# Layer 1's context stage placed between the shared and the routed experts, and statistics per tile in the last stage

## The chip, the cores and the metric

The kernel runs on one core of a Trainium2 chip. The metric is device time in microseconds (us) from launch to the end of the core's program; lower is better. A core has five engines that each run their own instructions in order: PE (matrix products, with a separate row PEld for its weight loads), DVE (vector), ACT (scalar functions), POOL (GpSimd) and SP (which here only starts transfers). They wait for each other through semaphores alone.

## The reference

Input: x, 64 sequences of 64 tokens of 128 features; a context of 64 tokens of 256 features per sequence (two halves of 128); a mask of patch lengths; two pairs of gates.

```python
x = x + tanh(g_xattn[0]) * attention(layernorm(x), context)
x = x + tanh(g_ffn[0])   * moe(layernorm(x))
x = x + tanh(g_xattn[1]) * depool(layernorm(x), context, mask)
x = x + tanh(g_ffn[1])   * linear_experts(layernorm(x))
```

- attention: 16 heads of 8 features over 64 own and 64 context keys, softmax, projection.
- moe: a shared gated FFN (128 to 256 and back), plus the one best of 8 experts of the same shape per token, fed with the token times the sigmoid of its best logit.
- depool: rmsnorm(x) times W_in plus b_in, plus a row of a decaying sum over the rms-normalised first half of the context (the rms is over all 256 features); which row is the token's "plug", a running count of patch ends that comes from the mask.
- linear_experts: the sum of the two best of 8 matrices applied to the token, and their biases.

## The kernel before

The program is written without a scheduler: each engine's order stands in the code, and every wait is put in by hand. The 4096 tokens are NT = 32 tiles of 128 tokens (two sequences). A stage is a pipeline: `walk` (L64) calls a step function that asks `stage(lag)` for the tile that is `lag` steps behind the newest, so one step of an engine touches several tiles at different points. The first steps and the drain are unrolled, the rest is a loop. A semaphore S[...] counts the tiles that have passed a point; `done()` waits for a tile, `freed()` for a buffer to be free again.

The stages in order of time, with their place in the profiled execution:

1. **Attention**, to 280 us. It takes 32 steps and a drain of 11 (the pipeline's depth is 11). It ends per tile with layer 0's second layernorm (the result is kept in VALL, which is XN2), its transpose (XNT) and the 8 router logits (LG). In a step ACT does in this order: copy onT of an older tile (L564), copy qc (L568), four exponentials (L557), copies xrT and XNT (L603, L604), and last, copy oS (L614). PE waits for onT (`pe.wait on_kept`) ahead of both the logits product L1129 and the projection L1132, and behind these stand the scores L1075 that the next exponentials read.
2. **Sort**, 280 to 292 us, on DVE from L844: best expert, its rank among the tokens of the same expert, and so a row of a buffer in which each expert's tokens stand together (NS = 40 tiles of 128 rows). ACT takes sigmoids and scales the 32 tiles (L631).
3. **Scatter and shared FFN**, 292 to 357 us. POOL issues one indirect DMA per tile (L466) that writes its rows to the sorted place. Beside it the shared FFN runs on 8 chunks of 4 tiles: PE lifts a chunk (L1206, L1207: four products of 128x512), ACT takes silu (L640), DVE multiplies (L890), PE takes it down (L1216: eight 128x128 products), DVE adds it to X (L895). In the same steps ACT squares the context, 8 activations a chunk (L646), whose sums are the rms. DVE compares patch ends with places (L900) and POOL turns them to plugs (from L487), writes them out and reads them back over 64 rows.
4. **Routed experts**, 357 to 447 us: 40 sorted tiles; SP loads (L368) and stores (L371), PE transposes (L1239) and multiplies (L1234 and others).
5. **Gather and context stage**, 447 to 519 us. POOL issues 32 indirect DMAs (L514) that fetch each tile's rows back. Beside it, per tile: DVE scales the context by its rms (L936), PE applies the decay (L1271), ACT copies the result (L674), DVE compares the plugs with the row number (L941, a 128x128 matrix of zeros and ones), PE picks with it (L1277), DVE adds the bias into DP, which is CV (L945); then DVE adds the gathered tile to X (L949) and takes its mean and variance (L955, L959), which ACT copies for the next step (L678).
6. **Root chain**, 519 to 522 us: once all 32 tiles have their moments, DVE forms the roots' arguments (L974 and on), ACT takes Sqrt (L682, with a table load), DVE inverts and refines.
7. **Last stage**, 522 to 652 us: 32 tiles, depth 9. ACT normalises (L690), PE multiplies by W_in (L1289), POOL adds DP (L527), DVE adds (L991) and takes moments; POOL takes variance and root (L531, L534), DVE normalises (L998), PE computes logits (L1309 with others); DVE finds the two best, PE applies all 8 experts (L1319) and DVE masks them (L1021); SP stores (L382).

SP also issues, after attention, the loads of all weights that are used later (L352) and five writes of zeros over the sorted buffer (L360); POOL multiplies these weights by their gates (L455 to L458) before the scatter.

## Time and profile before

| what | value |
|---|---|
| time, median of 3 runs | 609.88 us (608.68 to 610.11) |
| the profiled execution: its span | 652.3 us; no other time is given for it |
| PE busy / its weight loads | 535.1 us (82%) / 378.2 us (58%) |
| DVE busy | 426.2 us (65%) |
| ACT busy | 320.0 us (49%) |
| POOL busy | 247.1 us (38%) |

The page's slices of the span (16.3 us each; a digit is tenths of busy time, PEclk tenths of the full TensorE clock) show the stages: the sort is the gap in PE at slice 18, the gather the low PE values from slice 27 to 31.

```profile
PE   2699999999999999648638989995206479999998
DVE  4789898889898986375114323335218867888885
ACT  2477877777777776385234334442002442333320
POOL 5324444444444434378743700004760052232320
PEclk9799999999999999869868799998556859999999
```

The profile's rows are one execution, taken by the hardware profiler. A row of the timeline has the start in us from the span's start, the duration, the engine, the line, the operation, its output and input, how often, and in brackets the idle time before it and what ended it. "issue" and "remote" stand there when nothing in the program that the profile shows was waited for.

### The profile page before, as it was taken

What the parts mean: (1) busy time and instruction counts of PE and PEld (TensorE: products, weight loads), DVE (VectorE), ACT (ScalarE), POOL (GpSimd) and SP (SyncE); (2) the same over time, 40 slices, a digit from 0 to 9 for tenths busy, and PEclk for the clock granted to TensorE, in tenths of its full rate; (3) what the DMA queues carried; (4) which work ended last, traced back from release to release, by engine and by line L of the source; (5) the groups of instructions that cost most, each with busy time, mean ns of one, the idle gap of its engine ahead of it and who ended that gap; (6) DMA issues with size and microseconds to landing.
All of it is one profiled execution on the core that took longest, in us unless ns stands there. A gap on an engine that the chain in (4) does not pass through costs nothing. (4 is left out here: it accounts for less than half of the span.)

```text
span 652.3 us, 19574 instructions
## 1 busy us (share of the span) xinstructions
PE 535.1 (82%) x5898; PEld 378.2 (58%) x5899; DVE 426.2 (65%) x1504; ACT 320.0 (49%) x1039; POOL 247.1 (38%) x551
## 2 busy tenths in 40 slices
PE   2699999999999999648638989995206479999998
PEld 1366666666666666415325545554105359999997
DVE  4789898889898986375114323335218867888885
ACT  2477877777777776385234334442002442333320
POOL 5324444444444434378743700004760052232320
PEclk9799999999999999869868799998556859999999
DMA  8400000000000000821110252211110000000000
GB/s 278 168 4 3 4 3 4 1 1 1 1 1 1 1 2 4 325 85 45 52 49 6 52 115 64 67 53 41 52 52 0 0 2 14 21 16 20 16 22 25
DMA packets 24188, 27.24 MB, mean 42 GB/s; under 512 B 5144, under 2 KB 20816, under 8 KB 23504
## 3 DMA queue, kind: packets, MB, share of 16 engines
q1 hardware_dynamic: 21712, 21.40, 10.0%
q0 software_dynamic: 2432, 5.28, 3.2%
q8 instruction: 24, 0.39, 0.3%
q14 instruction: 20, 0.16, 0.1%
HBM read 17.06 MB, written 9.45 MB: 41 GB/s over the span
## 5 line engine op out<-in xcount | busy, mean ns | idle before, releaser
L740 DVE TENSOR_REDUCE negm<-PS 128x4 f16<-128x512 f32 x128 | 85.3, 687 | 2.3 <-PE PS L1062 1.3
L557 ACT ACTIVATE pexp<-PS 128x512 f32<-128x512 f32 x128 | 79.0, 625 | 7.3 <-PE PS L1075 6.7
L1319 PE MATMUL PS<-w,vp 128*128 128x128 f32 x512 | 64.3, 280 | 0.0
L514 POOL DMA_INDIRECT VALL<-sorted_y,posu x32 | 30.5, 953 | 83.5 <-DMA sorted_y<-arena 74.1
L1319 PEld LDWEIGHTS PS<-w,vp 128*128 128x128 f32 x512 | 61.4, 196 | 0.1
L1062 PE MATMUL PS<-kt,arena 128*64 128x128 f16 x1024 | 53.7, 229 | 5.7 <-DVE negm L740 5.1
L1089 PE MATMUL PS<-pexp,vp 128*32 128x64 f32 x2048 | 54.1, 225 | 2.8 <-ACT pexp L557 0.2
L923 DVE TENSOR_TENSOR pexp<-PS,oS 128x256 f32<-128x256 f32 x40 | 17.0, 424 | 55.5 <-ACT oS L656 55.5
L406 POOL TENSOR_TENSOR ve<-mv,epsc 128x1 f32<-128x1 f32 x32 | 6.4, 199 | 120.0 <-DVE mv L775 120.0
L1234 PE MATMUL PS<-rgu,xsT 128*128 x80 | 46.7, 667 | 3.5 <-ACT xsT L661 2.0
L1062 PEld LDWEIGHTS PS<-kt,arena 128*64 128x64 f16 x1024 | 33.3, 111 | 27.6 <-issue 11.8
L1089 PEld LDWEIGHTS PS<-pexp,vp 128*32 128x32 f32 x2048 | 34.3, 109 | 22.6 <-issue 11.9
L1075 PE MATMUL PS<-arena,kt 128*128 128x256 f16 x256 | 44.5, 276 | 0.0
L1271 PE MATMUL PS<-stack,cst 128*128 128x128 f32 x64 | 18.4, 380 | 31.0 <-DVE stack L936 16.6
L466 POOL DMA_INDIRECT sorted_x<-VALL,posu x32 | 34.0, 1063 | 13.9 <-issue 13.9
L1021 DVE TENSOR_TENSOR vp<-PS,xnT 128x1024 f32<-128x1024 f32 x32 | 38.7, 1209 | 0.8 <-PE PS L1296 0.8
L789 DVE COPY arena<-qc 32x512 f16<-32x512 f16 x128 | 37.0, 289 | 1.3
L1097 PE MATMUL PS<-ident,stack 128*128 128x128 f16 x384 | 34.2, 228 | 2.6 <-DVE stack L804 2.6
L704 ACT CAST mask1T<-PS 8x128 f32<-8x128 f16 x32 | 8.1, 254 | 55.7 <-PE PS L1324 55.7
L531 POOL TENSOR_TENSOR ve<-mv,epsc 128x1 f32<-128x1 f32 x32 | 6.1, 189 | 71.1 <-DVE mv L1012 71.1
L1271 PEld LDWEIGHTS PS<-stack,cst 128*128 128x128 f32 x64 | 11.9, 234 | 36.1 <-DVE stack L936 20.2
L568 ACT COPY qc<-PS 128x512 f16<-128x512 f16 x32 | 18.7, 585 | 27.8 <-PE PS L1097 27.8
(204 smaller groups left out, 1363.6 us busy)
## 6 DMA issues: line engine op xcount, KB each, us to landing
sorted_x<-zeros SPq DMA_DIRECT2D x5, 512.0 KB, 10.1
xs<-sorted_x SPq DMA_DIRECT2D x40, 64.0 KB, 1.8
sorted_y<-arena SPq DMA_DIRECT2D x40, 64.0 KB, 1.6
arena<-mT SPq DMA_DIRECT2D x128, 1.0 KB
rgu<-in_rt_gate_up_dram SPq DMA_DIRECT2D x1, 2048.0 KB
out_dram<-X SPq DMA_DIRECT2D x32, 64.0 KB, 1.5
X<-in_x_dram SPq DMA_DIRECT2D x1, 1536.0 KB, 8.6
CK<-in_ctx_k_dram SPq DMA_DIRECT2D x1, 1536.0 KB, 11.8
```

Source lines behind the costliest of these rows:

```text
L466: pool.indirect_dma_start(out=sorted_x, out_offset=bass.IndirectOffsetOnAxis(ap=posu[:, t:t + 1], axis=0), in_=XN2[:, t * D:t * D + D], in ...
L514: pool.indirect_dma_start(out=XN2[:, t * D:t * D + D], out_offset=None, in_=sorted_y, in_offset=bass.IndirectOffsetOnAxis(ap=posu[:, t:t + ...
L557: nc.scalar.activation(pexp[:, j, :], PS[:, 2 + j % 2, :], ACT.Exp).then_inc(S["exped"], 1)
L740: dve.tensor_reduce(negm[:, a.par, :, j], PS[:, j % 2, :].rearrange("p (h k) -> p h k", h=HG), AX.X, ALU.max, negate=True).then_inc(S["max ...
L789: last = dve.tensor_copy(qbd[rows, s.slot, :, hg, :], qc[rows])
L1021: dve.tensor_tensor(z[:, m.par], PS[:, 4:6, :].rearrange("p b (e t) -> p (b e) t", t=P), xnT4[:, m.slot, :].unsqueeze(1).to_broadcast([P, ...
L1062: last = nc.tensor.matmul(PS[64 * b:64 * b + 64, j % 2, hg * P:hg * P + P], qbd[:, a.slot, j, hg, 64 * b:64 * b + 64], kt[:, a.slot, b, j, :],
L1075: last = nc.tensor.matmul(PS[:, 2 + j % 2, 256 * g2:256 * g2 + 256], kt[:, b.slot, seq, g, :], qbd[:, b.slot, g, :, SEQ * seq:SEQ * seq + ...
L1089: last = nc.tensor.matmul(PS[32 * hg:32 * hg + 32, 7, g * P + SEQ * seq:g * P + SEQ * seq + SEQ], vp[:, b.par, seq, g * HG + hg, :], pexp[ ...
L1097: last = nc.tensor.transpose(bank16(bank)[:, col + g * P:col + (g + 1) * P], stack[:, s.par, w, g * HG:g * HG + HG, :].rearrange("p h c -> ...
L1234: nc.tensor.matmul(PS[:, 2 + s.par, :], xsT[:, s.par, :], rgu[:, ds(e_lift * (2 * FF), 2 * FF)], start=True, stop=True).then_inc(S["e_lift ...
L1319: nc.tensor.matmul(PS[:, 6 + y.par, 0:D], z[:, y.par, e, :], w1[:, e * D:e * D + D], start=(e == 0), stop=False)
```

## The change

1. The 11 late loads and the five zero writes go from SP (after attention) to POOL, at the end of its attention steps for tiles 2 to 11: two loads a step, and in the first five a zero write. The bias and the gain of the context's halves are now loaded four times side by side (ginit4, binB4), so there are 17 loads. Five small memsets are added at POOL's start.
2. The gates are multiplied into the weights by DVE, in the last attention steps and, for the small ones, in shared step 5. POOL's block of it is gone.
3. The 64 squares go from the shared stage to ACT's attention drain, 8 at the end of each of 8 steps. POOL's chain from squares to 1/rms goes ahead of the scatter.
4. The shared stage is unrolled on PE, DVE and ACT. The comparison of ends and places is made in two halves, the reduction over it is spread over steps 2 and 3, the plugs come from one scan on DVE in step 4, and SP writes and reads them.
5. The context stage runs on 4 tiles a step, between the shared stage and the routed experts: ACT scales four tiles, PE applies the decay to 512 columns at once, DVE multiplies by ginit4 on the way out (L964), compares in two halves (L954), PE picks (four products), DVE adds binB4 (L967).
6. The last stage has depth 12. POOL adds the gathered tile to X (it still issues all 32 gathers ahead of that); DVE takes the moments; POOL makes variance, root and shift for both norms of a step (four operations on 128x2 values), in place of the chain of stage 6 of the list above; ACT normalises for the second norm too (before: DVE, L998).

```diff
@@ sync
-            for dst, src in ((shd, sh_down), (rgu, rt_gate_up), ... (b1, expert_b)):
-                sp.dma_start(dst[:], src).then_inc(late_in, 16)
-            for c in range(NS // 8):
-                sp.dma_start(sx[c], zeros[:]).then_inc(zeroed, 16)
+            sp.wait_ge(plug_step, 2)
+            sp.dma_start(plugs, pm[:, 3, :]).then_inc(plug_out, 16)
+            sp.wait_ge(plug_out, 16)
+            for q in range(PAIRS):
+                sp.dma_start(plug[rows]..., plugs...to_broadcast([SEQ, NT, SEQ])).then_inc(plug_in, 16)
@@ gpsimd, attention step
+                if l and l.turn is None and 2 <= l.n < 12:
+                    for dst, src in late_loads[2 * l.n - 4:2 * l.n - 2]:
+                        pool.dma_start(dst[:], src).then_inc(late_in, 16)
+                    if l.n < 2 + NS // 8:
+                        pool.dma_start(sx[l.n - 2], zeros[:]).then_inc(zeroed, 16)
@@ gpsimd, after attention
-            pool.wait_ge(late_in, 16 * 11)
-            for w, k in ((shd, 2), (rdn, 2), (binB, 1), (ginit, 1), (w1, 3)):
-                pool.tensor_scalar(w[:], w[:], tgate[:, k:k + 1], None, ALU.mult).then_inc(late_ready, 1)
+            pool.wait_ge(squared, 2 * NT)
+            for q in range(PAIRS):
+                pool.dma_start(ssv[..., 1, :], ssv[..., 0, :]).then_inc(swap_in, 16)
...
+            pool.tensor_tensor(crms[:], crms[:], halfneg[:].to_broadcast([P, NT]), ALU.pow).then_inc(crms_step, 1)
@@ gpsimd, after the last gather
             def last_step(stage):
-                f, a = stage(1), stage(3)
+                x, v, f, a = (stage(i) for i in (0, 2, 4, 6))
+                if x:
+                    pool.wait_ge(S["l_y_in"], x.done())
+                    pool.tensor_tensor(X[:, x.cols(D)], X[:, x.cols(D)], XN2[:, x.cols(D)], ALU.add)
+                if v or a:
+                    pool.tensor_tensor(vv[:, par, both], mm[:, par, both, 1], two_eps[:, both], ALU.add)
+                    pool.tensor_tensor(nm[:, par, both], mm[:, par, both, 0], minus[:, both], ALU.mult)
+                    pool.tensor_tensor(roots[:, par, both], vv[:, par, both], halves[:, both], ALU.pow)
+                    pool.tensor_tensor(shifts[:, par, both], nm[:, par, both], roots[:, par, both], ALU.mult)
@@ scalar, attention step, after the copy of oS
+                if c and c.turn is None and NT - 9 <= c.n < NT - 1:
+                    square_four(c.n - (NT - 9))
@@ scalar, after the shared stage
+            for c in range(NC):
...
+                act.wait_ge(S["c_depooled"], l.freed())
+                for q in range(CT):
+                    last = nc.scalar.activation(hp[...], CK[...], ACT.Copy, scale=crms[:, t:t + 1])
@@ vector, attention step, behind the copy of the logits of tiles 28, 29, 30
+                    dve.wait_ge(late_in, 16 * 17)
+                    for w, k in weights_to_gate[g.n]:
+                        dve.tensor_scalar(w[:], w[:], tgate[:, k:k + 1], None, ALU.mult).then_inc(late_ready, 1)
@@ vector, after the shared stage
+            def context_step(stage):
+                l, f, a = (stage(i) for i in range(3))
+                if l:
+                    if l.n == 0:
+                        dve.wait_ge(plug_in, 32)
+                        dve.wait_ge(zeroed, 16 * (NS // 8))
...
+                if f:
+                    dve.tensor_tensor(dp[:, f.par, :], PS[:, f.par, :], ginit4[:], ALU.mult).then_inc(S["c_dp_kept"], 1)
+                if a:
+                    dve.tensor_tensor(DP[...], PS[:, 2 + a.par, :], binB4[:], ALU.add).then_inc(S["c_put"], 1)
@@ tensor, after the shared stage
+                    nc.tensor.matmul(PS[:, f.par, :], decay, hp[:, f.par, :], start=True, stop=True)
...
+                    for q in range(CT):
+                        last = nc.tensor.matmul(PS[:, 2 + s.par, at], pick[:, s.par, at], dp[:, s.par, at], ...)
+            pe.wait_ge(late_ready, 5)
+            pe.wait_ge(S["c_put"], Tile(NC - 1).done())
```

Two places of the order. **ACT in attention's drain**, one step from the copy of oS to the next exponentials. Before:

```order
L557 ACTIVATE pexp<-PS 128x512
L614 COPY oS<-PS 128x512
L564 COPY onT<-PS 128x128
L568 COPY qc<-PS 128x512
L557 ACTIVATE pexp<-PS 128x512 x2
```

And the same place now:

```order
L552 ACTIVATE pexp<-PS 128x512
L609 COPY oS<-PS 128x512
L618 ACTIVATE sqj,ssk<-CK 128x128
L618 ACTIVATE sqj,ssv<-CV 128x128
L618 ACTIVATE sqj,ssk<-CK 128x128
L618 ACTIVATE sqj,ssv<-CV 128x128
L618 ACTIVATE sqj,ssk<-CK 128x128
L618 ACTIVATE sqj,ssv<-CV 128x128
L618 ACTIVATE sqj,ssk<-CK 128x128
L618 ACTIVATE sqj,ssv<-CV 128x128
L559 COPY onT<-PS 128x128
L563 COPY qc<-PS 128x512
```

Eight squares stand between the copies of oS and onT (before: L614 and L564, now L609 and L559).

**PE between the last shared chunk and the first sorted tile.** The down products of the last two chunks (between them the loop's branch, L76), then the first transposition of a sorted tile (L1239). Before:

```order
L1216 MATMUL PS<-shd,pexp 128x128 x8
L76 REGISTER_ALU
L76 COMPARE_AND_BRANCH
L1216 MATMUL PS<-shd,pexp 128x128 x8
L1239 MATMUL PS<-cst,xs 128x128
L1251 TENSOR_LOAD texp
```

Now, with oS holding the scaled context, the first cst the decay matrix, pexp the depooled tiles and zeros the picks:

```order
L1219 MATMUL PS<-shd,pexp 128x128 x16
L1232 MATMUL PS<-oS,cst 128x512 x2
L1240 MATMUL PS<-pexp,zeros 128x128 x4
L1232 MATMUL PS<-oS,cst 128x512
L1240 MATMUL PS<-pexp,zeros 128x128 x4
```

and so on for each group of four tiles, until it ends with

```order
L1232 MATMUL PS<-oS,cst 128x512
L1240 MATMUL PS<-pexp,zeros 128x128 x8
L1265 MATMUL PS<-cst,xs 128x128
L1277 TENSOR_LOAD texp
```

Eight decay products and 32 picks now stand ahead of the first sorted tile; before, 32 and 32 of them (L1271, L1277) stood behind the last.

## Rows read from the trace of the kernel before

**Rows 1.** The page, its first line.

```profile
span 652.3 us, 19574 instructions
```

**Rows 2.** Busy time in five stretches: us, each engine busy (x instructions), granted clock, DMA share, GB/s.

```profile
243.00:280.00 37.00, 27.86 (x433) 18.51 (x431) 17.24 (x60) 18.85 (x50) 14.40 (x40) 0.88 0.48 177
...
272.00:276.00 4.00, 2.32 (x6) 1.36 (x6) 0.83 (x4) 0.87 (x5) 1.65 (x6) 0.50 0.89 330
...
357.00:447.00 90.00, 80.74 (x364) 47.85 (x364) 30.02 (x92) 37.06 (x122) 12.66 (x21) 0.96 0.28 68
...
447.00:489.00 42.00, 11.60 (x46) 8.68 (x46) 11.32 (x48) 3.92 (x17) 30.50 (x32) 0.56 0.19 50
...
522.00:652.00 130.00, 124.42 (x1056) 111.05 (x1056) 100.62 (x416) 38.05 (x128) 37.23 (x96) 0.93 0.06 17
```

**Rows 3.** Timeline: two long waits on nothing in the program, beside the scatter and the gather.

```profile
339.41 0.69 DVE L895 TENSOR_TENSOR X<-PS,X 128x512 f32 x1 [12.96 <-remote]
...
480.40 0.79 PE L1271 MATMUL PS<-stack,cst 128*128 128x128 f32 x2 [8.91 <-issue]
```

**Rows 4.** Timeline, PE: the shared stage's second and third chunk begin.

```profile
293.49 1.12 PE L1206 MATMUL PS<-XNT,shgu 128*128 128x512 f32 x2 [3.61 <-DVE pexp L890]
...
298.81 1.02 PE L1206 MATMUL PS<-XNT,shgu 128*128 x2
```

**Rows 5.** Timeline: first loads of sorted tiles, and the first routed transposition.

```profile
336.86 1.76 SPq L368 DMA_DIRECT2D xs<-sorted_x  x4
...
356.84 0.30 PE L1239 MATMUL PS<-cst,xs 128*128 128x128 f32 x1 [0.83 <-issue]
```

**Rows 6.** Timeline: last gather, last quad's first sum, last statistics, first normalised tile.

```profile
486.54 0.94 POOL L514 DMA_INDIRECT VALL<-sorted_y,posu  x1 [0.30 <-issue]
...
515.71 0.27 DVE L949 TENSOR_TENSOR X<-X,VALL 128x128 f32<-128x128 f32 x1
...
518.49 0.19 ACT L678 COPY mvl<-mv 128x2 f32<-128x2 f32 x1 [0.29 <-DVE mv L955]
...
521.76 0.88 ACT L690 ACTIVATE on<-X,mrr,rr 128x128 f32<-128x128 f32 x2 [1.54 <-DVE mrr L983]
```

**Rows 7.** Timeline, ACT: squares of the context's two halves in the shared stage.

```profile
292.92 0.31 ACT L646 ACTIVATE sqj<-CK 128x128 bf16<-128x128 f32 x1
...
293.21 0.31 ACT L646 ACTIVATE sqj<-CV 128x128 bf16<-128x128 f32 x1
```

**Rows 8.** Timeline, ACT and PE: one step of attention's drain.

```profile
249.47 0.58 ACT L614 COPY oS<-PS 128x512 f32<-128x512 f32 x1 [0.86 <-PE PS L1089]
...
250.04 0.27 ACT L564 COPY onT<-PS 128x128 f32<-128x128 f32 x1
...
250.38 0.43 PE L1129 MATMUL PS<-gatew,xrT 128*128 128x64 f32 x2
...
251.35 1.08 ACT L557 ACTIVATE pexp<-PS 128x512 f32<-128x512 f32 x2 [1.04 <-PE PS L1075]
```

**Rows 9.** Timeline, DVE: the pick of one tile; and the landing time of the places' reads.

```profile
498.62 0.27 DVE L941 TENSOR_SCALAR stack<-XNT,cst 128x128 f32 x1
...
DMA to landing us min/median/max: 8.1/9.1/10.2
```

**Rows 10.** POOL's waits between 60 and 130 us; its chain behind the squares.

```profile
POOL ve L406 <- DVE mv L775: 34.3, 9, 4.4
...
355.96 1.14 POOL L475 DMA_DIRECT2D ssv<-ssv  x2
...
359.19 5.50 POOL L483 TENSOR_TENSOR crms<-crms,halfneg 128x32 f32<-128x32 f32 x1
```

**Rows 11.** Timeline, DVE: the first step of the sort.

```profile
280.18 0.42 DVE L844 TENSOR_REDUCE top<-LG 128x32 f32<-128x256 f32 x1 [1.91 <-issue]
```

**Rows 12.** Timeline, PE: the expert products of two following tiles of the last stage.

```profile
618.38 1.95 PE L1319 MATMUL PS<-w,vp 128*128 128x128 f32 x16
...
621.99 1.95 PE L1319 MATMUL PS<-w,vp 128*128 128x128 f32 x16
```

More of the change, by code:

```diff
@@ L279, in flamingo_gated_two_layers @@
         scattered = sem("scattered")
[L280 removed]
+        for n in "gated lifted acted down added".split():
             S["h_" + n] = sem("h_" + n)
@@ L378, in store_out @@
             def store_out(stage):
-                o = stage(9)
+                o = stage(12)
                 if o:
@@ L640, in shared_step @@
                         nc.scalar.activation(sg[:, i, :], PS[:, 2 * i, :], ACT.Silu).then_inc(S["h_gated"], 1)
[L642 to L649 removed]
+            for c in range(NC):
+                shared_step(lambda lag: Tile(c - lag) if lag <= c else None)
+            for c in range(NC):
+                l = Tile(c)
+                if c == 0:
+                    act.wait_ge(crms_step, 3)
+                    act.wait_ge(S["h_acted"], Tile(NC - 1).done(2, 1))
+                act.wait_ge(S["c_depooled"], l.freed())
+                for q in range(CT):
+                    t = CT * c + q
+                    last = nc.scalar.activation(hp[:, l.par, q * D:q * D + D], CK[:, t * D:t * D + D], ACT.Copy,
+                                                scale=crms[:, t:t + 1])
+                last.then_inc(S["c_hp_ready"], 1)
             def sorted_step(stage):
@@ new lines, in _ @@
+            for c in range(NC + 1):
+                shared_step(lambda lag: Tile(c - lag) if 0 <= c - lag < NC else None)
+                if c < 2:
+                    all_pairs(c)
+                elif c == 2:
+                    any_of_half(32, 2)
+                    any_of_half(16, 3)
+                elif c == 3:
+                    any_of_half(8, 4)
+                    any_of_half(4, 5)
+                    any_of_half(2, 6)
+                    any_of_half(1, 7)
+                elif c == 4:
+                    places()
+                elif c == 5:
+                    dve.tensor_scalar(b1[:], b1[:], tgate[0:E, 3:4], None, ALU.mult).then_inc(bias_ready, 1)
+                    dve.tensor_scalar(gres[:], gres[:], (1 + EPS) ** -0.5, None, ALU.mult).then_inc(bias_ready, 1)
+                    dve.wait_ge(bias_ready, 2)
+                    dve.tensor_scalar(winT[:], winT[:], gres[:], tgate[:, 1:2], ALU.mult, ALU.mult)\
+                        .then_inc(bias_ready, 1)
@@ L915, in sorted_step @@
+            for c in range(NC + 2):
+                context_step(lambda lag: Tile(c - lag) if 0 <= c - lag < NC else None)
             def sorted_step(stage):
```

334 lines of the change are left out of this document (149 added, 185 removed).

## The prediction

> **What bounds the kernel now.** I read the busy time by stretches first, then the timeline at the seams, then the waits. [rows 2] The stages have different limits, so the page's shares over the whole span decide nothing. In attention's drain PE is busy 27.86 of 37 us; in the routed experts 80.74 of 90, in the last stage 124.42 of 130: PE sets these. In the gather, 447 to 489, PE is busy 11.6 and DVE 11.3 of 42 us, while POOL is busy 30.5: the stretch is as long as 32 indirect transfers take to be issued, and the context stage beside it is free.
>
> The profiled execution lasted 652.3 us [rows 1], the runs 609.9. The difference of 42.4 has to be placed before a sum can be made. [rows 3] Beside the scatter DVE stood 12.96 us and beside the gather PE 8.91 us on nothing that the program waits for. Without such stalls: the shared stage's chunks follow each other by 298.81 - 293.49 = 5.32 us [rows 4], so from 293.5 seven chunks and a last product and sum (2.6) end at 333.3. The scatter lets SP load the first sorted tiles at 336.86 [rows 5], and the first transposition would start some 2.4 us later, at 339.2; it started at 356.84: 17.6 us. [rows 6] The last gather is issued at 487.5; its landing (about 2) and the last quad's sum to last moments (518.68 - 515.71 = 3.0) would end at about 492.8, and ended at 518.7: 25.9 us. Together 43.5, and 652.3 - 43.5 = 608.8, against the median 609.88. So I take these stalls as the profiled execution's, and make the sum on the median: shared stage to 333.3, routed experts from 339.2 (scatter-bound), gather as long as POOL issues.
>
> **The change, part by part.**
>
> *Squares into the drain.* One takes 293.21 - 292.92 = 0.29 us [rows 7], eight 2.35, in each of eight steps: 18.8. They stand between the copy of oS and the copy of onT. [rows 8] In that step onT is copied at 250.04, right behind oS (249.47), PE's logits product that waits for it is at 250.38, and the next exponentials start at 251.35 after waiting 1.04 us for the scores that stand behind that product. So ACT's copy releases PE, and PE's scores release ACT: both are on the path there, and the squares go into it whole, less what slack ACT had (at most 0.35 in the first step, 0.1 in the second). I take 2.0 + 2.25 + 3 x 2.35 = 11.3 for the first five; in the last three ACT has little left to do and waits 1 us and more per copy, so 1.3 + 0.8 + 0.8. **+14.2.** Ends: ACT is busy 18.85 of 37 us, and 18.85 + 18.8 = 37.7, so if everything could shift freely they would cost 0.65; whole, 18.8. I take a value near the upper end since each step's chain has one round per engine.
>
> *Out of the shared stage.* PE sets its pitch (5.32), so ACT's relief is worth 0. POOL's chain behind the squares, 355.96 to 364.69 with the 5.50 us power in it [rows 10], is 8.7 us and now lies beside the 12 us of the sort: 0, unless the squares end late; then the scatter starts late, by at most what they overrun.
>
> *Context stage between shared and routed stage.* It has 8 steps. DVE does most: a 128x512 operation takes 0.69 us [rows 3], twice (0.60 to 0.69 each); a pick of 128x128 took 0.27 [rows 9], and two of 64 rows by 256 about 0.3 each: 1.85 us. ACT's four scaled copies are 1.2, PE's products about 1.3. So 8 x 1.85 + 1 of filling, from 333.3 to about 349, and PE waits for the last put before the first sorted tile: 349.3 where it was 339.2. **+10.** Lower end +8 (operations at 0.60, and the start before the last sum); upper end +20: a step that goes ACT, PE, DVE, PE, DVE in single file, 2.9 us. The plugs have to be there at 333: found at about 316, written, and read with 8.1 to 10.2 us to landing [rows 9], at about 330. What is taken out of the gather window is worth 0, since POOL's 32 issues bound it.
>
> *End of the gather.* Before, from the last issue to the first normalised tile: 2.0 + 3.0 + (521.76 - 518.68 = 3.1) = 8.1 to 8.4 us [rows 6]. Now POOL goes straight on: three sums of 0.46, moments, four small operations (about 1.2 with the waits), 2.7. **-5.7** (-4 to -7). The pipeline is three steps deeper, its first and last steps light: +1 (0 to +3).
>
> *Last stage.* [rows 12] A tile takes 621.99 - 618.38 = 3.61 us, and PE is busy 124.42 of 130. POOL gets a sum and four operations instead of two, about 2.2 us a step; DVE loses a normalisation (0.27) and gets sum-less moments (0.4). Both stay under 3.61: 0 (0 to +4, if a chain of POOL's gets longer than a step's lag).
>
> *Late loads and zero writes onto POOL.* [rows 10] POOL waits 34.3 us for 9 moments in the stretch 60 to 130, up to 4.4 at a time, and a transfer's issue took 1.14 for two to about that for one. Two or three fit: +0.5 (0 to +8). The loads no longer run while PE ends attention, where the DMA share was 0.89 at 272 to 276 [rows 2], nor does the sort's first step wait 1.91 for its code [rows 11]: -1.5 (-2 to 0). Gates on DVE in the drain +0.3 (0 to +1.5), memsets +0.2.
>
> The Trainium skill ("SBUF — State Buffer", rules for kernel authors) speaks against this move: a transfer issued from GpSimd beside a DVE operation in its two-port modes is starved of descriptor writes, and should go from another queue. No row of attention shows a POOL transfer, so the trace neither bears it out nor denies it there.
>
> **Sum:** 14.2 + 10 - 5.7 + 1 + 0.5 - 1.5 + 0.3 + 0.2 = 19.0, on 609.9: **629 us**.
>
> **The rivals.**
>
> *R1, the squares are mostly hidden.* If ACT's other copies shift forward and only 2 to 4 us stay, the sum is 609.9 + 19 - 11 = 618. For it: ACT is half idle in the drain. Against: the row of 251.35, where ACT waited on scores that its own copy had released.
>
> *R2, the other side: faster.* The stalls of [rows 3] may be partly real in the runs too. Then beside the gather the before kernel's per-tile context loop (8 crossings of engines, 32 times) ends late, and the change, which has nothing there, saves that time. If all 25.9 us were real, 629 - 26 = 603. It decides from 19 us on. For it: the loop has 32 steps with five hand-overs, and was late by that much in the one execution shown. Against: the runs' median fits the stall-free working to 1.1 us, and if 25.9 were real, something else of the same size would have had to vanish.
>
> *R3, the clock.* [rows 2] In 272 to 276, where PE was busy 2.32 of 4 us, the granted clock was 0.50 (1.2 GHz), over the drain 0.88. With 14 us more in the same steps PE's share goes from 75% to some 55%, and the clock may fall earlier: half the drain's PE work, about 10 of 20 us, at half speed: 639. The Trainium skill ("TensorE: Matmul & The Clock Gate", Part 1) has a gate of two levels that follows how busy the engine has lately been, which would ask for the same.
>
> *R4, POOL's transfers held up.* If each of the 25 issues takes a microsecond or more beside DVE's work and POOL's waits don't cover it, attention's steps 2 to 11 stretch: +8, 637. By the skill's rule above this would be the case.
>
> *R5, the plugs late.* If the read lands 8 us late, DVE waits in the first context step with all behind it: 637.
>
> **How the numbers follow.** Forecast 0.60, with a range of its own of 617 to 640 (squares 0.65 to 18.8 around 14.2, context stage +8 to +20, the end of the gather +-1.5); R1 0.12; R2 0.12; R3 0.07; R4 0.06; R5 0.03. R2 is left out of the range below 613, and of the others about 0.05 above: 613 to 642 holds the rest, some 0.83. A measurement of this kernel can tell about 0.3% (1.8 us) from no change. Faster comes from R2 where over 20 us are real, 0.09; within 0.3% from R2 at 17 to 20 us, 0.03; slower the rest, 0.88.
>
> **What would show it.** In the changed profile: (1) in steps 32 to 39 PE's product behind onT waits for the copy behind eight squares, and the steps are 2 us longer; the sort starts about 14 us later than 280.18. (2) From the last shared sum to the first sorted transposition 16 us, DVE busy in most of it; wrong if below 10 or if DVE stands idle for the plugs. (3) From the last gather's issue to the first normalised tile under 3 us. (4) Last stage at 3.61 us a tile. (5) POOL in steps 2 to 11 still waits for DVE. The prediction falls if the squares' steps are no longer than before, or if the runs of the changed kernel lie under 609 although (1) and (2) hold; then the stalls were real.

## The result, and the profile after

The changed kernel took **644.27 us** in the median of 4 runs (643.17 to 645.13), the kernel before 610.0 beside it: a ratio of 1.057 (95% interval 1.055 to 1.059). Forecast were 629 us, with a range of 613 to 642: the result lies outside it. The direction was right, the size was not: 34 us instead of 19.

The page of the changed kernel, its first line and the slices of PE and its clock (16.0 us each):

```profile
span 641.4 us, 19139 instructions
...
PE   1799999999999997663799779999700169999998
...
PEclk9989999999999999665899989999955559999999
```

PEclk is at 6, 6 and 5 tenths in slices 17 to 19, the drain and the sort, and PE has all but nothing to do in the gather, slices 30 to 32.

The profiled execution spans 641.4 us and took 643.44, so 2 us lie around a span. The kernel before was profiled once more (the first experiment), with a span of 607.7 us. The two spans can be taken apart at the same landmarks. The changed kernel's timeline, first instruction of each stretch (columns as before):

```profile
300.31 0.42 DVE L851 TENSOR_REDUCE top<-LG 128x32 f32<-128x256 f32 x1 [1.73 <-issue]
...
353.84 0.69 DVE L902 TENSOR_TENSOR X<-PS,X 128x512 f32<-128x512 f32 x1 [1.09 <-PE PS L1219]
...
376.20 0.30 PE L1265 MATMUL PS<-cst,xs 128*128 128x128 f32 x1 [0.94 <-issue]
...
464.67 1.00 POOL L491 DMA_INDIRECT VALL<-sorted_y,posu  x1 [110.57 <-DMA sorted_y<-arena]
...
503.78 0.95 POOL L491 DMA_INDIRECT VALL<-sorted_y,posu  x1 [0.30 <-issue]
...
507.32 0.49 ACT L686 ACTIVATE on<-X,shifts,roots 128x128 f32<-128x128 f32 x1 [45.76 <-POOL shifts L523]
...
526.81 1.49 PE L1329 MATMUL PS<-w,vp 128*128 128x128 f32 x6
```

They are the start of the sort, the last sum of the shared stage, the first sorted tile, the first and last gather, the first normalised tile and the first expert product of the last stage. They answer to [rows 5, 6, 11]. The same places of the kernel before in its second profile:

```profile
280.18 0.42 DVE L844 TENSOR_REDUCE top<-LG 128x32 f32<-128x256 f32 x1 [1.92 <-issue]
...
334.57 0.69 DVE L895 TENSOR_TENSOR X<-PS,X 128x512 f32<-128x512 f32 x1 [0.96 <-PE PS L1216]
...
338.75 0.45 PE L1239 MATMUL PS<-cst,xs 128*128 128x128 f32 x1 [4.22 <-DMA xs<-sorted_x]
...
429.67 1.07 POOL L514 DMA_INDIRECT VALL<-sorted_y,posu  x1 [73.48 <-DMA sorted_y<-arena]
...
468.95 0.94 POOL L514 DMA_INDIRECT VALL<-sorted_y,posu  x1 [0.30 <-issue]
...
477.62 0.88 ACT L690 ACTIVATE on<-X,mrr,rr 128x128 f32<-128x128 f32 x2 [1.54 <-DVE mrr L983]
...
493.18 1.06 PE L1319 MATMUL PS<-w,vp 128*128 128x128 f32 x4
```

| stretch (us) | before | after | difference | forecast |
|---|---|---|---|---|
| launch to the sort's first instruction | 280.2 | 300.3 | +20.1 | +13.7 |
| to the first sorted tile | 58.6 | 75.9 | +17.3 | +10 |
| to the first gather | 90.9 | 88.5 | -2.4 | 0 |
| to the first normalised tile | 48.0 | 42.7 | -5.3 | -5.7 |
| to the first expert product | 15.6 | 19.5 | +3.9 | +1 |
| to the end | 114.5 | 114.6 | +0.1 | 0 |
| sum | 607.7 | 641.4 | +33.7 | +19 |

The forecast column adds the prediction's terms by place; 13.7 is the squares' 14.2 with the loads, the sort's fetch, the gates and the memsets. So three places hold the miss of 14.7 us: the drain (+6.4), the context stage (+7.3) and the filling of the last stage (+2.9). They make 16.6; the routed experts, 2.4 us shorter where the forecast had 0, hide part of that.

Of the signs that the prediction named, three came as written: from the end of the last gather's issue to the first normalised tile 2.6 us (under 3), the last stage at 3.61 us a tile, and the plugs in time. Two came in kind but larger: the sort starts 20.1 us later (14), and from the last shared sum to the first sorted tile it is 376.20 - 353.84 = 22.4 us (16).

### The profile page after: what moved, and what is told of

The parts are those of the page before. It is cut to its first block, busy times and chain, and to the rows that moved or that the text cites. A ratio compares the mean times of both kernels' runs of the same rounds, so it can differ in the third digit from the quotient of the medians.

```text
span 641.4 us, 19139 instructions
## 1 busy us (share of the span) xinstructions
PE 521.0 (81%) x5850; PEld 366.9 (57%) x5851; DVE 415.3 (65%) x1378; ACT 327.5 (51%) x1037; POOL 268.6 (42%) x665
## 4 chain that ended last, share of the span: by engine, by line
PE 69%; ACT 11%; issue 8%; POOL 7%; DVE 4%; ACTq 1%; DMA 1%; SPq 0%; DVEq 0%; POOLq 0%
PE PS L1329 9%; PE PS L1260 7%; PE PS L1065 5%; PE PS L1092 5%; POOL VALL L491 5%; PE PS L1166 5%; PE PS L1100 4%; PE PS L1078 4%; PE PS L1271 3%; ACT sqj L618 3%; ACT pexp L552 3%; PE PS L1306 2%; PE PS L1219 2%; PE PS L1338 2%; PE PS L1209 2%
## 5 line engine op out<-in xcount | busy, mean ns | idle before, releaser
L416 POOL TENSOR_TENSOR ve<-mv,epsc 128x1 f32<-128x1 f32 x32 | 6.4, 200 | 132.5 <-DVE mv L782 132.5
L1092 PE MATMUL PS<-pexp,vp 128*32 128x64 f32 x2048 | 55.6, 231 | 2.7 <-ACT pexp L552 0.2
L981 DVE TENSOR_TENSOR pexp<-PS,oS 128x256 f32<-128x256 f32 x40 | 17.0, 425 | 56.1 <-ACT oS L665 56.1
L1315 PE MATMUL PS<-cst,on 128*128 128x128 f32 x32 | 10.3, 323 | 49.1 <-ACT on L686 45.4
L1092 PEld LDWEIGHTS PS<-pexp,vp 128*32 128x32 f32 x2048 | 35.6, 112 | 23.3 <-issue 12.7
L1078 PE MATMUL PS<-arena,kt 128*128 128x256 f16 x256 | 46.3, 285 | 1.1 <-DMA arena<-mT 1.1
L686 ACT ACTIVATE on<-X,shifts,roots 128x128 f32 (+1 forms) x32 | 15.8, 493 | 56.0 <-POOL shifts L523 55.0
L486 POOL DMA_INDIRECT sorted_x<-VALL,posu x32 | 33.5, 1047 | 15.6 <-issue 9.4
L989 DVE BATCH_NORM_STATS2 st<-X 128x6 f32 (+1 forms) x32 | 9.1, 285 | 43.8 <-POOL X L501 43.0
L1315 PEld LDWEIGHTS PS<-cst,on 128*128 128x128 f32 x32 | 5.1, 160 | 50.4 <-issue 45.6
```

The lines of the kernel that those rows point to most:

```text
L486: pool.indirect_dma_start(out=sorted_x, out_offset=bass.IndirectOffsetOnAxis(ap=posu[:, t:t + 1], axis=0), in_=XN2[:, t * D:t * D + D], in ...
L1078: last = nc.tensor.matmul(PS[:, 2 + j % 2, 256 * g2:256 * g2 + 256], kt[:, b.slot, seq, g, :], qbd[:, b.slot, g, :, SEQ * seq:SEQ * seq + ...
L1092: last = nc.tensor.matmul(PS[32 * hg:32 * hg + 32, 7, g * P + SEQ * seq:g * P + SEQ * seq + SEQ], vp[:, b.par, seq, g * HG + hg, :], pexp[ ...
```

## The experiments

Each ran with the kernel before beside it on the same chip. The kernel before takes 608 to 610 us on some chips and 653 on others; where a number comes from the second kind, this is said.

**The kernel before, once more.** No edit.

> The kernel before once more, unchanged, for a second profiled execution. If the 12.96 and 8.91 us stalls and their like belong to the one execution shown, the span is about 608 us (the median less some 2 us), the first sorted tile's transposition starts at about 339 and the first normalised tile of the last stage at about 496. If they are partly real in every run, the span is above 615 and the stalls stand at the same places.

Measured: 609.81 us, span 607.7. The first sorted tile is at 338.75 (expected 339), the first normalised one at 477.62: my 496 had forgotten to take off the scatter's 17.6 us as well; in the stretch itself it stands 7.7 us behind the end of the last gather's issue, where 8.1 to 8.4 were worked out. The working of the prediction, which took 43.5 us of stalls out of a 652.3 us profile, is borne out for this chip.

**No squares.** This kernel leaves the squares out: the sums that the rms is made from are a constant, so its output is not the reference's.

```diff
-                if c and c.turn is None and NT - 9 <= c.n < NT - 1:
-                    square_four(c.n - (NT - 9))
...
-            pool.wait_ge(squared, 2 * NT)
...
+            pool.memset(ssk[:], 100.0)
+            pool.memset(ssv[:], 100.0)
```

> The changed kernel without the 64 squares: the two sums that the rms is made from are set to a constant at the start, so the context is scaled by one constant in place of its rms. Theory: the squares cost 20 us in attention's drain (about 13 as work queued between the copies of oS and onT, about 7 because PE, waiting for them, is given the lower clock from 257 us on). Expected 644.3 - 20 = 624 us, the granted clock 1.00 until about 264 as before, the sort from about 280. Rival: the drain is longer for another reason (weights multiplied by DVE there, the loads issued from POOL) and the squares are mostly hidden: 640 us, the sort still starts after 295.

Measured: 623.97 us (620.43 to 624.41), ratio to before 1.021 (1.017 to 1.025). The sort starts at 281.73, and the whole time is 20.3 us under the first measurement of the changed kernel. So the squares cost 300.3 - 281.7 = 18.6 us up to the sort and all the rest of the change there 1.5.

```profile
281.73 0.42 DVE L850 TENSOR_REDUCE top<-LG 128x32 f32<-128x256 f32 x1 [1.73 <-issue]
```

Executions of one kernel differ by about a microsecond in their start (the first copy of oS stands at 38.90 us in one profile of the kernel before and at 40.00 in the other). Counted from the copy of oS ahead of the first squares to the sort, a measure without that, it is 38.2 us before, 56.9 in the changed kernel and 37.5 without squares: the squares cost 19.4 there.

**The same squares, other places in the same steps.**

```diff
-                    square_four(c.n - (NT - 9))        # 8 behind the copy of oS
...
+                squares(c, 2)      # behind the copies of onT and qc
...
+                squares(c, 1)      # ahead of the third exponential
...
+                squares(c, 3)      # ahead of the copy of oS
...
+                squares(c, 2)      # behind the copy of oS
```

> The same 8 squares in each of the same 8 steps, but put where ACT waits for PE: two behind the copies of onT and qc, one ahead of the third exponential, three ahead of the copy of oS, two behind it. Theory: what costs is their place between oS and onT, ACT has 2 to 3 us of idle time in a step: the drain's extra time falls from 20 to 5 us (3 to 9): 629 us. Rival: ACT's total work sets the drain (18.85 + 18.8 us in 37), so the place does not matter: 640 us or more.

Measured: 630.04 us (629.63 to 630.40), sort at 286.91: 13.4 of the 18.6 us come back with no work left out.

```profile
286.91 0.42 DVE L858 TENSOR_REDUCE top<-LG 128x32 f32<-128x256 f32 x1 [1.73 <-issue]
```

So it is not ACT's total work that costs. Two of the eight still stand between the copies of oS and onT; two squares of 0.29 us in 8 steps are 4.7 us, close to the 5.2 that stay. That the place alone does it, and not also that the eight stand in one block, was not tested apart. The chain of one step of the changed kernel's drain shows what the place does (timeline of ACT and PE):

```profile
270.46 0.59 ACT L609 COPY oS<-PS 128x512 f32<-128x512 f32 x1 [0.93 <-PE PS L1092]
...
270.94 0.31 ACT L618 ACTIVATE sqj<-CK 128x128 bf16<-128x128 f32 x1
...
273.29 0.25 ACT L559 COPY onT<-PS 128x128 f32<-128x128 f32 x1
...
273.59 0.69 PE L1132 MATMUL PS<-gatew,xrT 128*128 128x64 f32 x2 [2.76 <-ACT onT L559]
...
275.27 1.08 ACT L552 ACTIVATE pexp<-PS 128x512 f32<-128x512 f32 x2 [1.74 <-PE PS L1078]
```

Eight squares lie between 270.94 and 273.29, PE stands 2.76 us for the copy behind them, and then ACT stands 1.74 us for PE's scores. [rows 8] had the same chain with nothing in it and 1.04 us of ACT's wait; the growth to 1.74 is PE at the lower clock, as the next experiment shows.

**PE kept busy while it waits.** Two products of 128x384, whose result is not used, in each of the last five steps with a projection.

```diff
+                if m and m.turn is None and m.n >= NT - 5:
+                    if m.n == NT - 5:
+                        pe.wait_ge(S["v_kept"], Tile(NT - 1).done())
+                    for _ in range(2):
+                        nc.tensor.matmul(PS[:, 4, 0:3 * D], identf, wqkv[:], start=True, stop=True)
                 if m:
                     pe.wait_ge(S["on_kept"], m.done())
```

> The changed kernel, with two products of 128x384 in each of the last five attention steps with a projection, in the time in which PE waits for onT; their result is not used. Theory: the lower clock is a cost of its own, PE's work from 264 to 292 us is done partly at half speed. With PE kept busy the granted clock of that stretch rises from about 0.6 to 0.9 or more and the time falls by 3 to 6 us: 640 us. Rival: the wait for ACT alone sets these steps and the clock costs nothing: 644 us, or up to 3 us more for the added products.

Measured: 639.58 us (638.10 to 641.99); the sort starts at 295.96, 4.35 us earlier, although PE has more to do. Busy time and clock by stretches, of the changed kernel (length, PE, PEld, DVE, ACT and POOL busy, granted clock, DMA share, GB/s):

```profile
257.00:264.00 7.00, 4.20 (x83) 2.46 (x82) 1.80 (x5) 4.75 (x23) 1.91 (x7) 0.74 0.00 1
264.00:271.00 7.00, 6.49 (x83) 4.30 (x83) 1.69 (x7) 3.37 (x10) 2.19 (x8) 0.60 0.02 4
271.00:278.00 7.00, 4.27 (x45) 2.79 (x46) 1.14 (x5) 4.38 (x23) 1.14 (x4) 0.65 0.00 0
```

and with PE kept busy:

```profile
257.00:264.00 7.00, 5.34 (x92) 3.34 (x93) 2.16 (x6) 5.22 (x25) 2.10 (x8) 1.00 0.02 3
264.00:271.00 7.00, 5.30 (x84) 3.07 (x82) 1.69 (x7) 5.64 (x25) 2.17 (x8) 1.00 0.02 4
271.00:278.00 7.00, 5.70 (x86) 3.52 (x86) 1.69 (x7) 4.92 (x21) 1.14 (x4) 1.00 0.01 2
```

The granted clock is the third number from the right: 0.74, 0.60, 0.65 against 1.00 throughout. The Trainium skill ("TensorE: Matmul & The Clock Gate", Part 1) has the clock follow how busy PE has lately been; the trace agrees: with the waits filled it stays at 1.00. The same steps, from one copy of oS to the next: without squares,

```profile
256.36 0.59 ACT L610 COPY oS<-PS 128x512 f32<-128x512 f32 x1 [0.86 <-PE PS L1091]
...
261.70 0.59 ACT L610 COPY oS<-PS 128x512 f32<-128x512 f32 x1 [0.60 <-PE PS L1091]
```

in the changed kernel (the next copy is the 270.46 above),

```profile
261.03 0.59 ACT L609 COPY oS<-PS 128x512 f32<-128x512 f32 x1 [1.03 <-PE PS L1092]
```

and with PE kept busy, with ACT's wait for the scores in this step:

```profile
260.26 0.58 ACT L609 COPY oS<-PS 128x512 f32<-128x512 f32 x1 [0.86 <-PE PS L1092]
...
264.35 1.08 ACT L552 ACTIVATE pexp<-PS 128x512 f32<-128x512 f32 x2 [1.02 <-PE PS L1078]
...
267.99 0.58 ACT L609 COPY oS<-PS 128x512 f32<-128x512 f32 x1 [0.61 <-PE PS L1092]
```

| one step of the drain (us), from the first with squares | 1 | 2 | 3 | 4 |
|---|---|---|---|---|
| without squares | 6.41 | 5.70 | 5.34 | 5.33 |
| squares, PE kept busy | 8.36 | 7.92 | 7.73 | 7.66 |
| squares | 8.36 | 9.22 | 9.43 | 9.78 |

At clock 1.00 a step is 2.0 to 2.4 us longer, which is the eight squares; below it 3.5 to 4.5. So the lower clock, which the waits had brought about, is a cost of its own: 4.3 us of the 18.6, or 4.9 of the 19.4, and the roughly 14 left are the queue itself. The split is a subtraction and not exact: the added products kept the clock up until 278 us, while without squares it is 0.50 from 271 on as well.

**The squares alone, in the kernel before.** The edit puts the squares where the change has them and takes them out of the shared stage.

```diff
+                if c and c.turn is None and NT - 9 <= c.n < NT - 1:
+                    square_four(c.n - (NT - 9))
...
-                            nc.scalar.activation(sqj[:, k, :], ..., ACT.Square, accum_out=ss)   # shared stage
```

> The kernel before with one part of the change: the 64 squares in attention's drain, 8 behind the copy of oS in each of 8 steps, and none in the shared stage. Theory: they cost there what leaving them out of the changed kernel gave back, 18.6 us, whatever else is changed: 610 + 19 = 629 us, or 653 + 19 = 672. Rival: in the kernel before the drain has room, since DVE does not multiply weights there: under 620, or 663.

Measured: 626.34 us (625.81 to 631.35) beside 608.41, ratio 1.032 (1.027 to 1.036): 17.9 us, the sort at 296.89. From the copy of oS ahead of them to the sort it is 56.1 us against 38.2, the same 17.9: the squares carry their price with them, and the shared stage gives nothing back for it.

**The order in DVE's context step.**

```diff
             def context_step(stage):
...
+                if f:   # dp = depooled * ginit4
                 if l:   # the picks
-                if f:   # dp = depooled * ginit4
                 if a:   # DP = placed + binB4
```

> The changed kernel with one swap in DVE's context step: it takes the depooled tiles of the group before (the multiplication by the gain) first and the picks of the next group behind it. Theory: a step takes 2.7 us because DVE's picks wait for PE to have placed the group two before, and PE's placing waits for the multiplication that stands behind the picks; so pick, multiplication and placing run in single file. Swapped, DVE's own 2.1 us set the step: 7 x 0.6 = 4 us less, 640 us. Rival: PE's decay product and picks (1.0 + 1.1 us with their hand-overs) set it: no change, 644.

Measured, on a chip where the kernel before takes 653: 652.99 us, ratio 0.998 (0.995 to 1.001); the changed kernel takes 657.72 on another chip of that kind (below). Once more, where it takes 610:

> The changed kernel with the multiplication ahead of the picks in DVE's context step, once more. From the last shared sum to the first sorted tile 16.5 us instead of 22 in either case: 639 us where the kernel before takes 610, 653 where it takes 653.

Measured: 639.04 us (638.68 to 639.58), 5.2 less than the changed kernel's 644.26 on the same chip. From the last shared sum (355.35) to the first sorted tile it is 17.2 us in place of 22.4, the same 5.2. The changed kernel's timeline of DVE and PE in one step:

```profile
360.59 0.71 DVE L954 TENSOR_SCALAR zeros<-arena,cst 64x256 f32<-64x256 f32 x2 [0.67 <-PE PS L1240]
361.34 0.69 DVE L964 TENSOR_TENSOR pexp<-PS,ginit 128x512 f32<-128x512 f32 x1
...
361.94 0.68 DVE L967 TENSOR_TENSOR CV<-PS,binB 128x512 f32<-128x512 f32 x1
362.13 1.13 PE L1240 MATMUL PS<-pexp,zeros 128*128 128x128 f32 x8 [0.71 <-issue]
...
363.30 0.71 DVE L954 TENSOR_SCALAR zeros<-arena,cst 64x256 f32<-64x256 f32 x2 [0.67 <-PE PS L1240]
```

The picks wait for PE's placing (0.67), the multiplication stands behind the picks, the placing waits for the multiplication: 363.30 - 360.59 = 2.71 us a step. With the multiplication first:

```profile
360.60 0.70 DVE L960 TENSOR_SCALAR zeros<-arena,cst 64x256 f32<-64x256 f32 x2
361.34 0.69 DVE L967 TENSOR_TENSOR CV<-PS,binB 128x512 f32<-128x512 f32 x1
361.94 0.68 DVE L952 TENSOR_TENSOR pexp<-PS,ginit 128x512 f32<-128x512 f32 x1
362.54 0.70 DVE L960 TENSOR_SCALAR zeros<-arena,cst 64x256 f32<-64x256 f32 x2
```

1.94 us, with no wait left: about what the prediction had taken (1.85) for the order of the changed kernel.

**The changed kernel again, and the context stage beside the gathers.** The changed kernel was run beside two sets of kernels.

> The changed kernel itself once more, beside kernels that are to be compared with it. Where the kernel before takes 610 us, 644 as before. Where it takes 653 us (as beside the last four kernels), the stalls beside the scatter stay (17 us) and those beside the gather have nothing left to hold up: 644 + 14 = 658 us, so that the change costs 5 us there and not 34.

Measured: 657.72 us beside 653.58, ratio 1.006 (1.003 to 1.009). On such a chip the change costs 4 us, not 34.

> The changed kernel beside the next three. Where the kernel before takes 610 us: 644. Where it takes 653: 658.

Measured: 644.26 us beside 608.41, ratio 1.059 (1.057 to 1.061), as the first time. The edit for the context stage: its three loops (ACT, PE, DVE) stand behind the routed experts, and the plugs go to XNT.

```diff
-        plug = arena[:, 0:NT * SEQ]
+        plug = XNT[:, 0:NT * SEQ]
...
+            sp.wait_ge(S["h_lifted"], Tile(NC // 2 - 1).done(2, 1))
...
             walk(pe, NS, 7, sorted_step)
...
+            for c in range(NC + 1):
+                context_step(...)
```

> The changed kernel with its context stage, still four tiles a step, put back behind the routed experts, beside the gathers (the plugs are read into the free half of XNT for that). Theory: between shared and routed experts the stage costs what stands between them, 17.3 us more than in the kernel before; beside the gathers its 22 us are free, since POOL takes 40 us to issue 32. Expected 644.3 - 17.3 = 627 us. Rival: the stage next to the gathers and the routed stage's end is slowed or slows them, so that less than half comes back: 636 or more.

> The changed kernel with its context stage, four tiles a step, beside the gathers, once more. Where the kernel before takes 610 us: its 22 us are free beside 40 us of gathers, 627. Where the kernel before takes 653 us: the stage is itself held up beside the gathers (47 us instead of 16 from first to last put in the run before this), 647. Rival: it is no better than the changed kernel in either.

Measured, both where the kernel before takes 653: 647.42 us (641.9 to 650.07) and 652.12 (648.81 to 652.98), the second beside the changed kernel's 657.72: 5.6 us less, not the 17.3 or the 11 expected. The first was not measured beside the changed kernel. The timeline of PE beside the gathers, from the second, says why:

```profile
472.45 1.13 PE L1285 MATMUL PS<-pexp,zeros 128*128 128x128 f32 x8 [2.26 <-issue]
...
485.11 2.05 PE L1285 MATMUL PS<-pexp,zeros 128*128 128x128 f32 x8 [9.92 <-issue]
...
506.12 2.04 PE L1285 MATMUL PS<-pexp,zeros 128*128 128x128 f32 x8 [17.26 <-issue]
```

These are the stalls of [rows 3], in the same company: a stage that runs while POOL issues indirect transfers back to back. The stage took 47 us and ended behind the gathers. Its worth where the kernel before takes 610 us was not measured alone.

**Is it the indirect transfers?** In this kernel each tile goes to the place of its own number, so the tokens are not sorted and the output is not the reference's.

```diff
-                pool.indirect_dma_start(out=sorted_x, out_offset=..., in_=XN2[:, t * D:t * D + D], ...)
+                pool.dma_start(sorted_x[t * P:t * P + P], XN2[:, t * D:t * D + D])
```

> The changed kernel with its 32 indirect transfers of the scatter replaced by 32 plain ones from the same queue (each tile goes to the place of its own number, so the tokens are not sorted). The scatter then ends before the shared stage in any case. Theory on the stalls where the kernel before takes 653 us: PE and DVE are held up, one instruction at a time, while POOL issues indirect transfers; without them the shared stage takes the 40 us that PE needs and not 57: 658 - 16 = 642 us. Rival: what holds PE up is something else of that chip in this stretch, and the time stays at 655 or more. Where the kernel before takes 610 us both expect 644, since the shared stage sets the end of this stretch there.

> The changed kernel with 32 plain transfers in place of the indirect ones of the scatter, once more, since the chip of the last four did not show the stalls. Where the kernel before takes 653 us: theory (POOL's indirect transfers hold up the others) 642; rival 655 or more. Where it takes 610: 644 either way.

Measured: 645.72 us beside 608.41 and 643.74 beside 609.6. It was the same chip both times, of the kind without stalls, so this tells nothing about them. What it does show: without the indirect scatter the time stays, so the scatter is not what bounds the changed kernel before its context stage. What holds the engines up on the other chips stays open.

**Gathers between the last stage's steps.**

```diff
-            for t in range(NT):
+            def gather(t):
                 pool.indirect_dma_start(...)
+            for t in range(8):
+                gather(t)
...
-            walk(pool, NT, 12, last_step)
+            for s in range(NT + 12):
+                last_step(...)
+                if s + 8 < NT:
+                    gather(s + 8)
```

> The changed kernel, with POOL issuing only 8 gathers ahead of its last stage and one more behind each of its next 24 steps. Theory: the last stage needs a gathered tile every 3.6 us, one takes 1.26 us to issue, and POOL's step takes 2.4 us: 24 x 1.26 = 30 us of waiting go, and POOL's steps grow to about PE's 3.6. Expected 616 us (613 to 620). Rival: POOL stands in the chain from moments to root, so each gather issued between lengthens that chain and the step: at 1 us a step, 638.

> The changed kernel with 8 gathers ahead of the last stage and 24 between its steps, once more. The run before this showed that the 8 gathers cost nothing but that the last stage's filling took 27.5 us instead of 19.5, since its light first steps now wait for POOL's sum, roots and a gather (3.6 us). So 28 us less and 8 us more: 20 us under the changed kernel, 624 where the kernel before takes 610, 640 where it takes 653. Rival: 30 us less than the changed kernel, 614.

Measured, where the kernel before takes 653: 639.89 us and 637.72, the second 20.0 us under the changed kernel. The first expectation missed the filling: from the first normalised tile to the first expert product 27.5 us in place of 19.5; the first steps are 3.1 to 3.4 us long there, each behind POOL's shifts, in place of 1.5 to 2.4. The second, made from that, was met (637.72 for 640). What this alone gives where the kernel before takes 610 us was not measured.

**The parts together.** Squares in the shared stage, the context stage beside the gathers with the multiplication first, 16 gathers ahead of the last stage and 16 between its steps, in a first version from step 0 on, in a second from step 10 on. The edit from the first to the second:

```diff
             for s in range(NT + 12):
                 last_step(...)
-                if s + 16 < NT:
-                    gather(s + 16)
+                if s >= 10 and s - 10 + 16 < NT:
+                    gather(s - 10 + 16)
```

> A version made from these parts: squares in the shared stage (8 a chunk, POOL's chain behind the scatter), context stage of four tiles a step beside the gathers with the multiplication ahead of the picks, 16 gathers ahead of the last stage and 16 between its steps. If the prices add up: 644.3 - 18.6 (squares) - 17.3 (context) - 16 x 1.26 + 1 = 589 us, faster than both kernels. Rival: the context stage ends after the 16 gathers or the routed stage is slowed by the chain: 600 us.

> Squares in the shared stage, context stage of four tiles a step beside the gathers with the multiplication ahead of the picks, 16 gathers ahead of the last stage and 16 from its tenth step on, so that the filling is not slowed. Where the kernel before takes 610 us: 644.3 - 18.6 - 17.3 - 20 + 2 = 590 us, faster than both kernels. Where it takes 653 us: 5 us under the version with the gathers from the first step (623), 618. Rival: the prices do not add, since the context stage is now as long as the 16 gathers: 600 us.

> The version with squares in the shared stage, context stage beside the gathers and 16 of the gathers from the last stage's tenth step on, once more. Where the kernel before takes 610 us: 590 (585 to 596), since neither the shared stage nor the context stage is held up. Where it takes 653: 614.

Measured: 623.35 and 613.67 us beside 653 (one of the four runs of the second took 1114.13 us, and why is not known; the other three took 612.22 to 613.68); and **586.65 us** (584.06 to 587.87) beside 608.41, ratio 0.964 (0.962 to 0.966). This beats both kernels on both kinds of chip. Its timeline:

```profile
425.84 1.12 POOL L492 DMA_INDIRECT VALL<-sorted_y,posu  x1 [82.88 <-DMA sorted_y<-arena]
...
443.16 0.69 DVE L985 TENSOR_TENSOR CV<-PS,binB 128x512 f32<-128x512 f32 x1 [0.67 <-PE PS L1290]
...
448.61 0.49 ACT L691 ACTIVATE on<-X,shifts,roots 128x128 f32<-128x128 f32 x1 [11.08 <-POOL shifts L527]
...
467.94 1.27 PE L1335 MATMUL PS<-w,vp 128*128 128x128 f32 x5
```

The context stage ends 18 us behind the first gather, within the 16 that are issued by then; the last stage begins after 22.8 us where the changed kernel needs 42.7, and fills in 19.3.

## Why the prediction was right in direction and wrong in size

**The squares (forecast +14.2, measured +18.6).** The mechanism held: ACT's copy of onT queues behind eight squares, PE behind the copy, the next exponentials behind PE. The queue's own part came out as summed: 2.0, 2.2, 2.4 and 2.3 us in the first four steps at clock 1.00 (worked out 2.0, 2.25 and then 2.35 each), and some 14 in all. What failed is that R3 was held to be another case (0.07) instead of a consequence of the first: the prediction's own chain makes PE idle in every step, and the granted clock fell to 0.74 from 257 us on, where the kernel before still has 1.00. It priced that at 10 us; it is 4.3 to 4.9.

**The context stage (+10, measured +17.3).** The step that failed is "8 x 1.85": DVE's work was counted and the order of its waits was not. The step measured 2.71 us, close to the 2.9 that the prediction named as its upper end, though by a shorter ring than the one it named: picks, multiplication and placing between DVE and PE, without ACT. Eight steps at 0.86 us more are 6.9 of the 7.3 us. The order stood in the code: pick(c) waits for placed(c-2), which waits for the multiplication behind the pick before. With the order turned, the measured step is 1.94 us. The plugs (R5) were in time.

So both large terms came out near their upper ends, 18.6 of 18.8 and 17.3 of 20. The two upper ends together would give 629 + 4.6 + 10 = 643.6; the stated range ended at 642.

**End of the gather (-5.7, measured -5.3)** and **last stage (0, measured +0.1)** were right. (Behind the last gather's issue it was 7.7 us and is 2.6; the other 0.2 are in the gathers.) **The filling (+1, measured +3.9)** was mis-sized: not for three more steps, since there are 8 steps between the first normalised tile and the first expert product in both kernels. Each of them now waits for POOL's chain of sum, roots and shift; the first three take 1.5 to 1.9 us, the others about 2.4, as two following starts of ACT's normalisation show. Before, the mean was 1.95 (15.6 / 8), now it is 2.44.

```profile
514.67 0.49 ACT L686 ACTIVATE on<-X,shifts,roots 128x128 f32<-128x128 f32 x1 [1.73 <-POOL shifts L523]
...
517.05 0.49 ACT L686 ACTIVATE on<-X,shifts,roots 128x128 f32<-128x128 f32 x1 [1.35 <-POOL shifts L523]
```

**The small terms.** The sort's first instruction still waits 1.73 us [rows 11: 1.91], so it is not the late loads that delay it. The 1.5 us taken off came in part: without squares the drain from the copy of oS on is 0.7 us shorter than before. What eats that up lies ahead of the first copy of oS, which stands at 40.3 to 41.2 us in the changed kernel and those made from it, against 38.9 and 40.0 in the two profiles of the kernel before; more than the 0.2 us for the memsets, but hardly beyond the scatter of the starts, and its cause was not looked for. POOL's transfers in attention cost nothing that the trace shows: from the first copy of oS to the last it is 225.8 us in the kernel before and 225.9 without squares. There are 22 of them (17 loads and 5 writes), not the 25 of the prediction's R4. The Trainium skill ("SBUF — State Buffer", rules for kernel authors) asks to issue a transfer from ACT or SP where it runs beside DVE in its 2x or 4x modes; whether DVE was in one there, no trace here shows. The 2 MB load from POOL landed in 7.9 us, and R4 did not come true. Elsewhere an issue did take longer beside DVE: in the second profile of the kernel before, one of the 32 scatter transfers took 4.87 us to issue instead of 0.96, while DVE ran its comparison of 64x4096 values for 4.41 us. The routed stage became 2.4 us shorter, which no step had: luck for the sum. The granted clock over it was 0.96 instead of 0.94, which points the same way; its cause was not tested.

**R1 (618)** is out: the drain gives the squares no room where they stand. **R2, the other side,** was judged too simply. The stalls of [rows 3] were neither in every run nor of one profile only: they stand in every run on some chips. Where they occur, the kernel before takes 653 us and the changed one 657.7. There the change costs 4 us instead of 34, 30 us less. Its context stage no longer stands beside the gathers: from the end of the last gather's issue to the first normalised tile it is 2.6 us there too, against 34.3 in the first profile of the kernel before. R2's mechanism is real on those chips (it had 25.9 us), and the change is still not faster. On the chips of the first measurement they don't occur, and the working on the median held.

## What to carry to other kernels

When an in-order engine waits for a copy and the copying engine waits for it in turn, work put between the two is paid in full, and here again in the matrix engine's clock; the same work spread over the places where the copying engine waits anyway cost under a third. A stage's step is the longest ring of waits in its code order, not the largest sum of work on one engine: write the ring down before counting. And before moving a stage out of a stretch that another engine bounds, ask what it will push where it goes: here it left 40 us of cover, free on the chips without stalls, for a place on the path, while the real lever was to let the bounding engine's transfers run between the steps of the next stage.

## What was not expected of the hardware

The same kernel takes 610 us on some chips of the same kind and 653 on others, in every one of its runs there (7 runs on one chip and 13 on another of the first kind, 13 and 16 runs on two chips of the second; each of the two was measured on one occasion only, so the occasion may be part of it). The 44 us are waits on nothing in the program (up to 17.34 us for PE, and 21.17 for DVE in the second version of the parts together); the long ones stand beside POOL's back-to-back indirect transfers, which is not yet shown to be their cause; with the last stage's own steps between the gathers the last stage kept its filling time (19.3 us in the second version of the parts together, on such a chip). A difference of 5% between two kernels can so be nothing on one chip and all on another.
